# Score matmuls issued as couples of a plain and a shifted head, ScalarE's PSUM reads moved ahead of each exponential, and near-bank fills moved to other eighths of a step

## The reference

```
def _mha(q_in, k_in, v_in, Wq, Wk, Wv, bv, causal):        # 16 heads of 16
    q, k, v = q_in @ Wq, k_in @ Wk, v_in @ Wv + bv
    scores = einsum('bhse,bhte->bhst', q, k) * 0.25
    if causal: scores = where(tril, scores, -inf)
    return softmax(scores) @ v
x = layernorm(x)
x = layernorm(_mha(x, x, x, ..., causal=True) + x)          # first layer
x = layernorm(_mha(x, ctx, ctx, ..., causal=False) + x)     # second layer
```

## Time and profile before

| what | us |
|---|---|
| median of 3 runs | 1558.11 (1557.0 to 1561.98) |
| the profiled execution's own time | 1571.12 |
| span of its profile | 1569.4 |
| the decoder in it | about 33 to 421 |
| steps of causal items (from QUERY to QUERY) | 21.7 to 25.5, and 30.9 for the one with TABLE |
| steps of plain items | 20.49 |

### The profile page before, as it was taken

How to read it: one execution, slowest core, us unless ns; L and a number is a source line. 1 busy time by engine, 2 the same in 40 slices (tenths; PEclk the granted TensorE clock), 3 DMA queues, 4 the chain that set the end, 5 groups by cost and what they waited for, 6 DMA issues and landing times. The chain is left out here.

```text
span 1569.4 us, 26159 instructions
## 1 busy us (share of the span) xinstructions
PE 1153.9 (74%) x9362; PEld 767.7 (49%) x9362; DVE 975.9 (62%) x2633; ACT 613.1 (39%) x1214; POOL 463.6 (30%) x616
## 2 busy tenths in 40 slices
PE   2687767777499710788888888820599997699998
PEld 1364444444278610677777777720254543345454
DVE  4645566777247530788888888834465652477776
ACT  1334455666355201566566656500154443000000
POOL 4234554323426644133333333355110100100000
PEclk9777898999789855899999999965586876799999
DMA  6323222322023234565666556245121210101000
GB/s 187 106 58 98 68 86 83 124 79 62 20 82 117 92 120 177 212 234 211 206 231 239 202 208 233 72 129 174 56 59 46 74 31 28 55 27 34 26 9 14
DMA packets 130245, 171.35 MB, mean 109 GB/s; under 512 B 13747, under 2 KB 104646, under 8 KB 127174
## 3 DMA queue, kind: packets, MB, share of 16 engines
q1 hardware_dynamic: 126534, 160.77, 31.3%
q0 software_dynamic: 3584, 8.92, 1.8%
HBM read 123.31 MB, written 46.14 MB: 108 GB/s over the span
## 5 line engine op out<-in xcount | busy, mean ns | idle before, releaser
L1972 PE MATMUL moe_ps_u<-moe_x_hl,moe_up_hl 128*128 128x256 f16 x1932 | 226.5, 276 | 68.8 <-DVE moe_up_hl L2048 42.6
L1972 PEld LDWEIGHTS moe_ps_u<-moe_x_hl,moe_up_hl 128*128 128x128 f16 x1932 | 184.5, 99 | 110.8 <-DVE moe_up_hl L2048 49.1
L2335 PE MATMUL mix_ps_e<-wr_hl,mix_u_hl 128*128 128x512 f16 x768 | 172.4, 380 | 0.0
L2092 POOL CAST moe_mid_hl<-moe_mid 128x256 f16<-128x256 f32 x161 | 71.8, 446 | 291.8 <-DVE moe_mid L2063 291.8
L2048 DVE SCALAR_TENSOR_TENSOR moe_up_hl<-moe_up_in,moe_up_hl 128x512 f16<-128x512 f32 x161 | 123.3, 799 | 54.4 <-ACT moe_up_hl L2021 54.4
L542 ACT ACTIVATE dec_probs<-dec_ps_t 128x768 f32<-128x768 f32 (+1 forms) x128 | 117.2, 917 | 83.3 <-PE dec_ps_t L444 83.1
L2447 DVE SCALAR_TENSOR_TENSOR mix_acc<-mix_ps_e,mix_shares,mix_acc 128x256 f32<-128x256 f32 x256 | 110.3, 477 | 39.0 <-PE mix_ps_e L2335 38.7
L1294 DVE TENSOR_REDUCE memory_neg_m<-memory_ps_s 128x2 f32<-128x512 f32 x128 | 84.8, 689 | 66.2 <-PE memory_ps_s L1071 63.5
L2021 ACT ACTIVATE moe_up_hl<-moe_up_in 128x512 f16<-128x512 f32 x161 | 99.2, 619 | 62.0 <-DMA moe_up_in<-in_moe_w 62.0
L431 PE MATMUL dec_ps_s<-dec_k_st,dec_q_st 48*128 48x256 f16 (+1 forms) x512 | 51.5, 281 | 90.6 <-DVE dec_neg_m L640 47.1
L2335 PEld LDWEIGHTS mix_ps_e<-wr_hl,mix_u_hl 128*128 128x128 f16 x768 | 74.8, 98 | 83.4 <-issue 1.1
(11 more groups left out here) (278 smaller groups left out, 2101.1 us busy)
## 6 DMA issues: line engine op xcount, KB each, us to landing
moe_up_in<-in_moe_w SPq DMA_DIRECT2D x23, 1792.0 KB, 7.6
moe_down_in<-in_moe_w SPq DMA_DIRECT2D x23, 896.0 KB, 4.7
moe_raw<-in_mix_wr SPq DMA_DIRECT2D x32, 256.0 KB, 7.7
dec_q_dram<-dec_q_hl SPq DMA_DIRECT2D x48, 128.0 KB, 2.0
dec_k_dram<-dec_k_hl SPq DMA_DIRECT2D x48, 128.0 KB, 2.0
dec_q_st<-dec_q_dram SPq DMA_DIRECT2D x64, 96.0 KB, 2.5
dec_k_st<-dec_k_dram SPq DMA_DIRECT2D x64, 96.0 KB, 2.6
xs<-zeros SPq DMA_DIRECT2D x8, 736.0 KB
```

The source lines that it names most:

```text
L1972: mm = nc.tensor.matmul(bank[:, m, :], up_hl[t.slot][:, w, m, dc, f * P:(f + 1) * P], x_hl[t.slot][:, x, dc, :], start=(dc == 0 and w == x ...
L2335: mm = nc.tensor.matmul(ps_e[fill % RING][:, :, :], u_hl[t.slot][:, r, dc, k * P:(k + 1) * P], wr_hl[:, m, dc, 2 * q:2 * q + 2, :], start= ...
```

## The change

Four things change, all in the decoder.

1. **Couples.** `pair_of_scores` and `pair_of_shifted` (four plain matmuls of an even and an odd head of nxt, then four shifted ones of item t) become two calls of `both_scores` in an eighth. The call j issues the plain matmuls of head 2p+j of nxt alternating with the shifted matmuls of head 2p+1-j of t. One call stands at the front of the eighth and one at its end, with the fills of the eighth between them. `s_filled` now counts heads and not pairs; `t_filled` still counts pairs.
2. **ScalarE.** In each eighth the copies out of the near and far banks stand ahead of `exponentials(t, p)` and no longer behind it.
3. **Near fills.** VALUE moves from eighth 5 to 6, TABLE from 6 to 4, and TURN from eighth 0 of the step to eighth 7 of the step before (hence `ahead` = t+3 and one more empty step at the front, `LEAD` 3). QUERY and KEY stay at 1 and 2.
4. **VectorE's code** is written in another order, but its instructions come in the same order as before, except `finish_table`, which moves from the end of eighth 7 to the end of eighth 5. GpSimd's order is unchanged. ScalarE's `high_part` of a weight piece moves from eighth 6 to 4.

```diff
-                for kind, n, at in ((TURN, new, 0), (QUERY, new, 1), (KEY, new, 2), (VALUE, nxt, 5)):
+                for kind, n, at in ((QUERY, new, 1), (KEY, new, 2), (VALUE, nxt, 6), (TURN, ahead, 7)):
...
-                def pair_of_scores(n, p):
-                    for j in range(2):
-                        scores_ready(n, 2 * p + j)
-                    for k in range(TT):
-                        for j in range(2):
-                            mm = scores(n, 2 * p + j, k)
-                    mm.then_inc(s_filled, 1)
...
+                def both_scores(t, p, j):
+                    nxt, plain, other = t + 1, 2 * p + j, 2 * p + 1 - j
+                    if within(nxt):
+                        scores_ready(nxt, plain)
+                    if within(t):
+                        shifted_ready(t, other)
+                    for k in range(TT):
+                        if within(nxt):
+                            mm = scores(nxt, plain, k)
+                            if k == TT - 1:
+                                mm.then_inc(s_filled, 1)
+                        if within(t):
+                            mm = shifted_scores(t, other, k)
+                            if k == TT - 1 and j == 1:
+                                mm.then_inc(t_filled, 1)
...
-                        if within(nxt):
-                            pair_of_scores(nxt, p)
-                        if within(t):
-                            pair_of_shifted(t, p)
+                        both_scores(t, p, 0)
...
-                        if p == 5 and within(nxt):
+                        if p == 6 and within(nxt):
                             project_values(nxt)
-                        if p == 6 and t == TABLE_AT:
-                            memory_rows()
+                        if p == 7 and within(ahead):
+                            turn_rows(ahead)
+                        both_scores(t, p, 1)
...
-                        if within(t):
-                            exponentials(t, p)
                         if p == 0 and within(old):
                             copy_outputs(old, GROUPS - 1)
...
+                        if p == 7 and within(ahead):
+                            rows_high(ahead)
+                        if within(t):
+                            exponentials(t, p)
...
-                    dve.wait_ge(s_filled, PAIRS * n + h // 2 + 1)
+                    dve.wait_ge(s_filled, HEADS * n + h + 1)
```

50 lines of the change are left out of this document (21 added, 29 removed).

## The result

The changed kernel took 1572.56 us in the median of four runs (1571.36 to 1575.38); the kernel before, run beside it, 1557.55 (1556.51 to 1561.98). The ratio is 1.0093, with a 95% interval of 1.0069 to 1.0118. The forecast was 1556, its range ended at 1570.

What follows compares the result with a forecast made beforehand. The bound was taken as the hand-over between engines in queue order. Step terms of +3.4 us and the clock's -5.4 gave -2.0, applied to the median 1558.1: 1556 us, range 1538 to 1570.

Steps and rivals of the forecast that it cites:

- The walk: Plain step followed fill to fill in the new order, each wait from unit prices; six links sum to +0.68 us.
- PV 2 to PV 3 +1.64: Plain step: PV 3 waits for the exponential of pair 7, now behind TURN's copy; link 3.44 us, was 1.80.
- KEY to PV 0 +1.32: Plain step: a couple behind KEY delays a maximum and then `divide`, which PV 0 needs; 3.27 us against 1.95.
- PV 3 to QUERY -2.69: Plain step: TURN is split long before, so QUERY follows sooner; 1.83 us against 4.52, the gain of the change.
- The causal step was given -0.24: Causal step by the same rules: +1.50, +0.76 and -2.50 us over its links; seven steps give -1.7 us.
- The two first steps were given -3.0: Two steps ahead of any PV 3 win without the waits: -1.5 us each, bounds 0 and -2.69 each.
- The last three steps have no TURN to take away but keep the late exponential and `divide`: Decoder's end: between 0 and +1.64 us a step, taken as +1.0 each, +3.0 in all.
- TABLE, given +1: Step with TABLE: same TensorE cost wherever it stands, readers delay VALUE by about 1 us; between 0 and +2.
- I take half of the excess back: -5.4: Ten slow QUERY fills, 10.8 us excess in all: half returns with the clock, -5.4 us, bounds 0 and -10.8.
- The clock did not come back in full: Rival: denser approach to QUERY regains the full clock and all 10.8 us; total -7.4 us, 1551; chance 0.20.
- The late `divide`: Rival: single-head hand-over removes the +1.32 and +0.61 us waits; 1536, or about 1540 with half; chance 0.14.
- The slower rival: Causal layer's PV 3: exponential of pair 7 costs 1.64 us, not 0.76, link about 4; +9.6 us, 1568; chance 0.26.

Runs made afterwards that it cites:

- e4: Changed kernel with both couples ahead of the fills and the exponential ahead of ScalarE's copies only from t = 14 on; 0.9925 of before, decoder's end 422.8 us.
- e10: e2 with ScalarE's exponential behind the copies of each eighth, as in the changed kernel; 0.9889 of before, decoder's end 401.5 us.
- e2: Changed kernel with both couples of each eighth ahead of its fills and the exponential ahead of ScalarE's copies; 0.9616 of before, decoder's end 366.9 us.
- e5: Changed kernel with TABLE back in eighth 6, its readers moving with it; 1.0035 of before, decoder's end 425.6 us.
- e1: Kernel before with only TURN moved, to eighth 7 of the step ahead; 0.9842 of before, decoder's end 395.3 us.
- e3: Changed kernel with VectorE's `divide` ahead of the odd head's maximum in eighths 2 and 6; 0.9887 of before, decoder's end 402.7 us.
- e8: e2 with TABLE back in eighth 6; 0.9622 of before, decoder's end 359.2 us.
- e11: e2 with `divide` ahead of the odd head's maximum, as in e3; 0.9614 of before, decoder's end 364.1 us.

## Why the prediction was wrong

**The steps that held.** The walk through the plain step, link by link, against the changed kernel's rows from 322.62 to 343.31:

| link | before | walk | measured |
|---|---|---|---|
| QUERY to KEY | 2.98 | 3.28 | 3.27 |
| KEY to PV 0 | 1.95 | 3.27 | 3.28 |
| PV 0 to PV 1 | 4.34 | 3.84 | 3.75 |
| PV 1 to PV 2 | 4.91 | 5.52 | 5.34 |
| PV 2 to PV 3 | 1.80 | 3.44 | 3.26 |
| PV 3 to QUERY | 4.52 | 1.83 | 1.79 |
| step | 20.49 | 21.18 | 20.69 |

The waits that it named stand where it put them: PV 0 and PV 2 for `divide` (1.27 us each), PV 3 for the exponential (1.05), TURN's 2.09 us stall gone. "PV 2 to PV 3 +1.64" came as +1.46, "KEY to PV 0 +1.32" as +1.33, "PV 3 to QUERY -2.69" as -2.73. Small errors of nearly one sign made the step +0.20 and not +0.68. The causal step was given -0.24 and came out at -0.29, and that is luck in part: against the second profile of before it is +0.07, and inside it TensorE's idle time fell by 3.1 us over the six steps while its matmuls took 1.4 longer, where the walk had their durations unchanged. The two first steps were given -3.0 and came out at -4.7.

**The steps that failed.** Three terms, each off by 5 us or more, make up the miss.

**"The last three steps have no TURN to take away but keep the late exponential and `divide` ... I take +1.0 each, +3.0."** Its bounds were 0 and +1.64 each, at most 4.9. The last three steps grew by 8.1, the whole stretch from QUERY 15 on by 10.3. Near fills run out there, so the gain of moving TURN is gone and nothing else replaces it, while each eighth still holds its second couple behind its fill. That much I had seen; what I took over without a walk was the size, from a link of a steady step. The waits for `divide` and for the exponential stay, TensorE has less between them, and the granted clock falls from 0.86 to 0.77 over the stretch: about 7.5 of the 10.3 us are longer matmuls. The term had no part for the clock. e4 shows that the place of the couples and of the exponentials together makes this loss: the two last steps in the other order, with the order of all ahead of them unchanged, give 12.6 us back. The couples weigh more: with them at the front and the exponential still behind the copies (e10) the end takes 57.6 us, against 68.9 in the changed kernel and 55.4 in e2.

**TABLE, given +1**, bounds 0 and +2. The step grew by 6.5. The clock falls to half 1.6 us into TABLE and stays there for the other 10.8 us of its 12.37; before, half clock covers 4.5 of its 9.30. TABLE lasts 3.1 longer and VALUE behind it 1.3 longer; the rest is nearly all waits, 2.4 us more of them, with 1.28 and 1.13 for `divide` and 0.92 for TABLE's readers among the new ones. The sentence "TABLE costs TensorE the same wherever it stands" was false: over all profiles it took 8.82 to 13.83 us, at a mean granted clock of 0.80 to 0.50. But the longer TABLE alone does not make the longer step. In e2 it takes 12.50 us in the new place and the step 30.67, in e10 13.19 and 31.75. So 5.6 of the 6.5 need the second couple behind the fills. e5 recovers 3.1 of it by TABLE's place; the two causes overlap.

**"I take half of the excess back: -5.4."** Ten QUERY fills of before had an excess of 10.8 us over 1.47 each. The same ten of the changed kernel last 2.74, 2.77, 1.76, 1.47, 1.47, 2.76, 2.77, 2.77, 2.65 and 2.24 us, an excess of 8.7: 2.1 came back. The second profile of before has an excess of 9.3, so even that is hardly a change. And all of TensorE's matmuls in the six causal steps together took longer, 105.1 us against 103.7, at a mean granted clock of 0.81 against 0.83: the term of -5.4 measured +1.4 in these steps. Two of ten became fast; "fewer than ten at over 2 us" was true, and the gain was not. The wait ahead of PV 3, which the prediction had at 1.3 to 1.7 us, is 1.66 in the row ahead of 210.41, and QUERY behind it is slow. e1 says what was taken wrongly: there the stall behind TURN is gone and no new wait stands ahead of PV 3, and TensorE's matmuls in the six causal steps take 93.6 us and not 103.7, though now VALUE is slow in five of them (2.00 to 2.74 us). I had credited the clock to the one stall that was removed, and priced it by QUERY's fills alone, at most 10.8 us in the whole decoder; from the changed kernel to e2 the matmuls of the six causal steps alone shrink by 15.3 us (105.1 to 89.8).

The Trainium skill (page "TensorE: Matmul & The Clock Gate", section "What's actually happening") has activity release the clock; the runs agree in direction, with 1.00 in e2, where TensorE is busy for 14.01 of 17.22 us, and 0.78 in the changed kernel, where it is busy for 18.15 of 24.16. They don't say where the line runs: the plain step of before, busy for 15.39 of 20.49, keeps 1.00.

**The whole, term by term** (decoder's end, the two first profiles): first steps with the stretch ahead of them -5.2, the step with TABLE +6.5, causal steps -1.7, the plain steps with the one between up to the cut at PV 3 +3.1 (0.9 and 2.2), the last three +8.1, sum +10.8, where the prediction had -2.0. The 12.8 us between the two come out as: the end 5.1 more than given, TABLE 5.5 more, the clock's -5.4 which is not there as a gain of its own, first steps 2.2 less, plain steps 1.0 less (+4.1 given).

**The rivals.** The clock did not come back in full. The late `divide` does not cost less than the walk says in its link (3.28 us from KEY to PV 0, walked 3.27); e3 shows that it costs more over the program, 30 us of decoder. The slower rival had the right sign and the wrong place: its link in the causal layer, PV 2 to PV 3, measured 3.55 us (205.10 to 208.65), as walked, and not the 4 from which it was to decide. That PV 3 there costs much more than its link says showed only in e10 and e2.

**What I missed beyond terms.** I priced the change against before, found gains and losses of 2 to 3 us a step in balance, and took the balance for the nature of the change. It was several changes: three good ones (TURN, single heads in place of pairs, VALUE's eighth, together about 4% by the ratios) and two bad ones (the second couple and the exponential behind the fills) that ate them. The walk held some of these parts: -2.69 for TURN, +1.64 for the exponential, +1.32 and +0.61 for `divide`, which one line of another order (e3) takes away. It gave nothing to single heads and to VALUE's eighth by themselves, and the rival that named the single-head hand-over put it in the place where the second couple stands behind the fill.

**Open.** e10 moved the exponential only where the couples stand at the front. What its order is worth in the changed kernel, where the last scores of an eighth come late anyway, was not tried. The chips of the batches differ, and differences of a few us of decoder between kernels of different batches (e2 against e8 and e11) I don't read. Why the clock falls in one plain step of e1 and not in another of the same order is open too, and so is what VALUE's eighth is worth when the couples stand behind the fills.

## What to carry to other kernels

An in-order queue passes a delay on: a producer placed behind a long fill holds back its consumer, and with it everything queued behind that consumer on the other engine, here `divide` and through it the bank for PV 0. Issue short producers ahead of the long fill, and split the prediction of a mixed change into its parts, since each can be walked, and run, alone.

Walk the last steps and the one-time jobs (here TABLE) as their own cases: what hides a wait in the steady step is not there at the end, and 16.8 of this kernel's 17.8 us of losses (10.3, 6.5 and 1.0) stood in those two places. Where the granted clock is below 1.00 in a stretch, or may come to be, bound a term by the durations at both levels (QUERY 1.47 and 2.77, PV 1.07 and 1.94; TABLE 8.82 at a mean of 0.80 and 13.83 at 0.50), because a wait can cost its own length and then the slower fills behind it. And price the clock by TensorE's busy time over the whole step, not by the fill that showed it first: in e1 QUERY became fast and VALUE slow.
